# Adapter columns placed beside the output weights, their split made tile by tile, and the gathers put behind the first stage's weights

## The chip, the cores and the metric

The kernel runs on one core of one Trainium2 chip. The metric is device time in microseconds (us), the median of three runs. A profile of one execution, taken by the hardware profiler, shows what every engine did and when: TensorE (PE; its weight loads are PEld), VectorE (DVE), ScalarE (ACT), GpSimd (POOL) and SyncE (SP, which here only issues DMAs).

## The reference

Four layers, each added to its input x of shape 8 x 128 x 512 (B=8 rows, T=128 tokens, HID=512). All is in fp32.

```python
x = x + einsum('bsi,boi->bso', x, weight[adapter_ids])       # L0: one 512x512 weight of 8 for each row
x = x + attention(x)                                         # L1: 32 query heads in 8 groups (g), D=128
x = x + (x @ B_sel^T) @ A_sel^T                              # L2: rank 16
x = x + x @ W^T + b + 2 * lora(x)                            # L3: rank 16
def lora_linear(x, w, a, b, ids):                            # q, k, v and the output of L1 are of this form
    return x @ w + (x @ a[ids]) @ b[ids]                     # w: 512 x 4096 (q), 512 x 1024 (k, v), 4096 x 512 (output)
...
q, k = apply_rope(q), apply_rope(k)
p = softmax(causal_mask(q k^T / sqrt(128)))
o = (p v).reshape(B, T, 4096)
return lora_linear(o, wo, ao, bo, ids)                       # ao: 8 x 4096 x 16, selected per row b
```

## The kernel before

Every fp32 product is made of three matmuls in the format fp32r: an operand is split into a high part (a ScalarE copy that rounds) and a low part (a subtraction on VectorE or GpSimd), and high x high, low x high and high x low are summed in PSUM.

The program has four stages, each a block with a barrier at its end.

**First stage** (to 99 us): for each row b, TensorE transposes x and the row's own weight (five tiles of 128x512, L275), ScalarE and VectorE split them, TensorE multiplies (L286 to L288), VectorE adds the result to `res`, TensorE turns x1 (L296) and computes the adapters' inner products (L307 to L309) and turns these (L319). SyncE issues the weight of row b (1 MB, L225) into one of two buffers when the tiles of row b-2 have been transposed (`tile_ready`), then x of row b+1 and three adapter loads. GpSimd issues the gathers of the rows' adapters from HBM to HBM: 16 of 64 KB for keys and values (`bkv_sel`, L249 and L250), then 16 of 256 KB for queries and the output (`bq_sel`, `ao_sel`, L254 and L255); it starts as soon as the ids are there, and its part of the block ends when all have landed. Behind row b=4 SyncE waits for the small gathers and loads the first block of the second stage.

**Second stage** (to 229 us): keys and values. **Third stage** (to 766.8 us): attention, 8 heads g (each a group of four query heads) by 8 tiles b, 64 slots t = 8g + b. In a slot TensorE does, in this order: scores of t, a quarter of the queries of half a head (L81 to L86), turn of t-1 (four transposes, L1059), outputs of t-2, values of t-1 (L1067 to L1069). The order is written by hand and is the same in the heads 1 to 6, which are one loop body.

`outputs` (L1070 to L1092) multiplies the tile's attention result by the head's slice of wo: four query heads by three matmuls of 512 columns into `ps_out` (L1081 to L1083; each loads a 128x128 piece of `ot_hi` or `ot_lo` as its weights). Eight more matmuls (L1090, L1091) multiply the adapter slice `ao_pack` (high and low part side by side, 32 columns, as weights) into `ps_ao`. VectorE adds `ps_out` to `res` (L975) and `ps_ao` to `axo` (L976).

The slice of wo comes once a head: ScalarE rounds it head by head into `wo_hi` in slot b=1 (L844), after the last tile of the head before has been read (`out_ready`); VectorE subtracts two quarters (L962, in slots b=1 and b=2), GpSimd the other two (L932, in slot b=1) and behind them the low part of `ao_pack` (L935). GpSimd's other work in a slot: normalizing probabilities (L922), adding the two halves of rotated queries (L915), and in slots 0 to 3 splitting query weights (L907).

**Fourth stage** (to the end): the output's adapter product, L2 and L3. It begins with four matmuls (L1243) that spread `axo` over the partitions with a 0/1 matrix, `row_gather`.

Of the kernel before, what the change touches and what calls it, by code (L numbers as in the profile page):

```python
# [7 lines left out]
P = 128  # L8
F32 = mybir.dt.float32
# [21 lines left out]
def program(nc, x, lora_ids, pos, attn_ids, slot_ids, mask, w0, wq, wk, wv, wo, aq, bq, ak, bk, av, bv, ao, bo,  # L31
            l2a, l2b, w3, b3, l3a, l3b, ident_c, causal_c, rope_c, gather_c, twin_c, out):
# [34 lines left out]
    with whole:  # L67
# [22 lines left out]
        res = sb(whole, "res", [P, B, HID])  # L90
        ident = sb(whole, "ident", [P, P])
        ident_r = sb(whole, "ident_r", [P, P], F32R)
        axo = sb(whole, "axo", [2 * R, B, T])
# [3 lines left out]

        row_gather = sb(whole, "row_gather", [2 * R, 2, P])
# [55 lines left out]
        with ExitStack() as c:  # L154
# [51 lines left out]
            with nc.Block() as block:  # L206
                @block.sync
                def _(sp):
                    sp.dma_start(id_rows[:, 0, :], lora_ids.rearrange("(a b) -> a b", a=1)).then_inc(lora_ids_in, 16)
                    sp.dma_start(res[:, 0, :], x[0]).then_inc(x_in[0], 16)  # L210
                    sp.wait_ge(lora_ids_in, 16)
                    for b in range(B):
# [13 lines left out]
                        if b + 1 < B:  # L226
                            sp.dma_start(res[:, b + 1, :], x[b + 1]).then_inc(x_in[b + 1], 16)
# [12 lines left out]
                def _(pool):  # L240
# [19 lines left out]
                def _(pe):  # L260
                    def transposes(b):
# [3 lines left out]
                        for j in range(TILES):  # L265
# [7 lines left out]
                            for n in range(KC):  # L273
                                src = res[:, b, n * P:(n + 1) * P] if j == 0 else w0_raw[b % 2][:, n, (j - 1) * P:j * P]
# [16 lines left out]
                    def turn_x1(b):  # L291
# [3 lines left out]
                        for k in range(KC):  # L295
                            mm = pe.transpose(ps_x1[:, k, :], res[:, b, k * P:(k + 1) * P], ident[:, :])  # L296
# [94 lines left out]
                def _(dve):  # L391
# [8 lines left out]
                    def add(b):  # L400
                        dve.wait_ge(y_ready, b + 1)
                        dve.tensor_tensor(res[:, b, :], ps_y[b % 2][:, :], res[:, b, :], ALU.add).then_inc(x1_done, 1)
# [12 lines left out]
                    def pack_ax(b):  # L415
# [3 lines left out]
                        dve.wait_ge(zeroed, i + 1)  # L419
# [60 lines left out]

                    for i in range(2):
# [28 lines left out]
        ao_in = sem(late, "ao_in")  # L510
# [12 lines left out]
        def load_wo(dma, g):  # L523
            dma.dma_start(wo_raw[:, :, :], wo[bass.DynSlice(g * GW, GW), :].rearrange("(h p) n -> p h n", p=P)).then_inc(wo_in, 16)
            for b in range(B):
                dma.dma_start(ao_raw[:, b, :, :], ao_sel[b, bass.DynSlice(g * GW, GW), :].rearrange("(h p) r -> p h r", p=P)).then_inc(ao_in, 16)
# [8 lines left out]
        with ExitStack() as c:  # L535
# [24 lines left out]
            with nc.Block() as block:  # L560
                @block.sync
                def _(sp):
                    sp.wait_ge(first_packs, PAIRS)
                    load_block_b(sp, 1)
                    for n in range(BLOCKS * UNITS):
# [26 lines left out]
                        if n == VU:  # L592
                            load_wo(sp, 0)
                        if n == VU + 4:
# [124 lines left out]
        with ExitStack() as c:  # L719

            wq_raw, bq_raw, wq_hi, wq_lo, bq_pack = raw_w, raw_b, blk_hi[0], blk_lo[0], blk_b[0]
            wo_hi = sb(c, "wo_hi", [P, G, HID], F32R)
            wo_lo = sb(c, "wo_lo", [P, G, HID], F32R)
            ao_pack = sb(c, "ao_pack", [P, B, G, 2, R], F32R)
# [17 lines left out]
            ps_out = ps(c, "ps_out", [P, HID])  # L742
            ps_ao = ps(c, "ps_ao", [P, 512])
# [25 lines left out]
            axo_done = sem(c, "axo_done")  # L769
# [8 lines left out]
            with nc.Block() as block:  # L778
                @block.sync
                def _(sp):  # L780
                    def slots(g):
                        sp.wait_ge(wo_lo_done, G // 2 * (g + 1))
                        sp.wait_ge(wo_lo_pool, G // 2 * (g + 1))
                        sp.wait_ge(ao_lo_done, g + 1)
# [5 lines left out]
                        load_kv(sp, g + 1, 0)  # L790
                        sp.wait_ge(s_ready, B * g + B)
# [22 lines left out]

# [3 lines left out]
                    sp.dma_start(row_gather[:, :, :], gather_c).then_inc(w3_in, 16)  # L818
# [13 lines left out]
                def _(act):  # L832
# [10 lines left out]
                    def wo_hi_part(g, h):  # L843
                        act.activation(wo_hi[:, h, :], wo_raw[:, h, :], ACT.Copy).then_inc(wo_hi_done, 1)  # L844

                    def ao_hi_part(g):
                        act.wait_ge(ao_in, 16 * B * (g + 1))
                        act.activation(ao_pack[:, :, :, 0, :], ao_raw[:, :, :, :], ACT.Copy).then_inc(ao_hi_done, 1)
# [13 lines left out]
                    def slots(g, first, last):  # L862
                        for b in range(B):
                            t = B * g + b
                            number = t if first else None
# [26 lines left out]
                            if b == 1:  # L892
                                wo_hi_part(g, 1)
                                wo_hi_part(g, 3)
                                ao_hi_part(g)

                    over_heads(act, slots)
                    pt(B * KVH - 1, None)
                    ot(B * KVH - 1, None)

                @block.gpsimd
                def _(pool):
# [13 lines left out]

                    def slots(g, first, last):
                        for b in range(B):
                            t = B * g + b
                            i = b % 2  # L920
                            pool.wait_ge(inv_done, t + 1)
# [6 lines left out]
                            if b == 1:  # L928
                                for h in range(G // 2, G):

                                    pool.wait_ge(wo_hi_done, G * g + 2 * (h - G // 2) + 2)
                                    pool.tensor_tensor(wo_lo[:, h, :], wo_raw[:, h, :], wo_hi[:, h, :].bitcast(F32),  # L932
                                                       ALU.subtract).then_inc(wo_lo_pool, 1)
                                pool.wait_ge(ao_hi_done, g + 1)
# [527 lines left out]
```

## Time and profile before

| | us |
|---|---|
| median of three runs (lowest to highest) | 832.05 (831.7 to 832.5) |
| the profiled execution: its time | 832.55 |
| its span, first to last instruction | 830.9 |
| TensorE busy in the span | 771.7 (93%) |
| VectorE, ScalarE, GpSimd busy | 541.9, 324.5, 283.2 |
| mean granted clock of TensorE | 0.973 |

The difference of time and span, 1.65 us, lies before the first and after the last instruction. Busy times are sums over stages with different limits; for a stretch, the windows give the busy time of each engine in it, and a timeline gives each instruction with the idle time of its engine before it in brackets, and what ended that. TensorE's matmuls are pipelined, so that their durations overlap: what one costs is read from start to start.

### The profile page before, as it was taken

To read this page: it belongs to the slowest core of one execution; us is meant where nothing else is said; L and a number is where in the kernel's file an instruction comes from. 1 tells how busy PE (TensorE), PEld (TensorE's weight loads), DVE (VectorE), ACT (ScalarE), POOL (GpSimd) and SP (SyncE) were. 2 spreads that over 40 slices of the span, in tenths; PEclk is the share of its full clock that TensorE was granted. 3 is DMA by queue.
4 is the path that set the end of the run, shared out by engine and by line. 5 is a ranking of instruction groups with operands and counts; after the bars stand their busy time and mean duration, and the time that the engine had idled before them with its cause. 6 is when DMAs were issued, how large, how long until landed. Compare 5 with 4: busy or idle time off the path is not lost. (4 is left out here: it accounts for less than half of the span.)

```text
span 830.9 us, 13659 instructions
## 1 busy us (share of the span) xinstructions
PE 771.7 (93%) x4280; PEld 645.1 (78%) x4280; DVE 541.9 (65%) x1428; ACT 324.5 (39%) x924; POOL 283.2 (34%) x261
## 2 busy tenths in 40 slices
PE   4588897999789999999999999999999999988898
PEld 3477785778578888888888888888888888875686
DVE  2579542588665767677667667676767666754883
ACT  3255432311063445345335345435434543432550
POOL 5300020034455236227236326334523622420320
PEclk9889799999989999999999999999999999999899
DMA  9992187886405124213404402602512210710502
GB/s 270 348 262 57 56 214 211 239 229 191 139 2 141 37 65 109 70 49 78 114 0 120 120 0 65 165 10 63 133 43 63 64 38 13 153 16 8 124 19 84
DMA packets 112748, 86.86 MB, mean 105 GB/s; under 512 B 60534, under 2 KB 79126, under 8 KB 112454
## 3 DMA queue, kind: packets, MB, share of 16 engines
q1 hardware_dynamic: 110770, 79.83, 35.7%
q0 software_dynamic: 1792, 6.49, 2.3%
q8 instruction: 19, 0.31, 0.2%
q14 instruction: 19, 0.16, 0.1%
q10 hardware_dynamic: 148, 0.07, 0.0%
HBM read 71.40 MB, written 20.73 MB: 111 GB/s over the span
## 5 line engine op out<-in xcount | busy, mean ns | idle before, releaser
L922 POOL TENSOR_TENSOR prob<-prob,rinv 128x512 f32<-128x512 f32 x64 | 66.6, 1041 | 214.5 <-DVE rinv L1008 214.5
L871 ACT ACTIVATE prob<-sm,nmax 128x128 f32<-128x128 f32 x256 | 99.7, 391 | 77.9 <-DVE nmax L993 77.9
L1081 PE MATMUL ps_out<-wo_hi,ot_hi 128*128 128x512 f32 x256 | 106.5, 416 | 4.3 <-DVE ot_lo L970 2.4
L915 POOL TENSOR_TENSOR qt<-qc,qs 128x512 f32<-128x512 f32 x60 | 77.8, 1297 | 94.3 <-DVE qs L951 94.3
L860 ACT ACTIVATE ot_hi<-ps_o 128x512 fp32r<-128x512 f32 x64 | 38.1, 595 | 163.4 <-PE ps_o L1069 163.4
L1082 PE MATMUL ps_out<-wo_lo,ot_hi 128*128 128x512 f32 x256 | 100.7, 393 | 0.0
L1083 PE MATMUL ps_out<-wo_hi,ot_lo 128*128 128x512 f32 x256 | 100.6, 393 | 0.0
L81 PE MATMUL ps_q<-x1t_hi,blk_hi 128*128 128x512 f32 x240 | 100.4, 418 | 0.0
L82 PE MATMUL ps_q<-x1t_lo,blk_hi 128*128 128x512 f32 x240 | 95.3, 397 | 0.0
L83 PE MATMUL ps_q<-x1t_hi,blk_lo 128*128 128x512 f32 x240 | 95.1, 396 | 0.0
L951 DVE TENSOR_TENSOR qs<-ps_q,sin_t 64x512 f32<-64x512 f32 x120 | 82.7, 689 | 3.7
L993 DVE CUSTOM_DVE_ANT_0 sm<-ps_s,maskbias 128x128 f32<-128x128 f32 x256 | 59.0, 286 | 34.1 <-issue 33.5
L1051 PEld LDWEIGHTS ps_s<-kt,qt 128*128 128x128 f32 x512 | 67.7, 193 | 10.8 <-issue 5.4
L1051 PE MATMUL ps_s<-kt,qt 128*128 128x128 f32 x512 | 68.4, 277 | 5.2 <-PEq L560 5.2
L1081 PEld LDWEIGHTS ps_out<-wo_hi,ot_hi 128*128 128x128 f32 x256 | 48.1, 188 | 14.9 <-DVE ot_lo L970 4.0
L1083 PEld LDWEIGHTS ps_out<-wo_hi,ot_lo 128*128 128x128 f32 x256 | 48.0, 188 | 11.4
L990 DVE MEMSET gate<- 128x1 f32 x64 | 3.8, 59 | 79.8 <-PE ps_s L1051 79.8
L1082 PEld LDWEIGHTS ps_out<-wo_lo,ot_hi 128*128 128x128 f32 x256 | 48.3, 189 | 8.6
L854 ACT ACTIVATE pt_hi<-ps_t 128x512 fp32r<-128x512 f32 x64 | 38.1, 595 | 41.4 <-PE ps_t L1059 41.4
L83 PEld LDWEIGHTS ps_q<-x1t_hi,blk_lo 128*128 128x128 f32 x240 | 45.4, 189 | 11.0
L966 DVE TENSOR_TENSOR pt_lo<-ps_t,pt_hi 128x512 fp32r<-128x512 f32 x64 | 44.2, 691 | 13.4 <-ACT pt_hi L854 11.9
L82 PEld LDWEIGHTS ps_q<-x1t_lo,blk_hi 128*128 128x128 f32 x240 | 45.6, 190 | 8.3
(201 smaller groups left out, 1757.8 us busy)
## 6 DMA issues: line engine op xcount, KB each, us to landing
wo_raw<-in_L_cond_wo SPq DMA_DIRECT2D x8, 1024.0 KB, 5.3
raw_w<-in_L_cond_wq SPq DMA_DIRECT2D x8, 1024.0 KB, 6.5
w_raw<-in_L_cond_weight SPq DMA_DIRECT2D x7, 1024.0 KB, 6.9
raw_b<-bq_sel SPq DMA_DIRECT2D x56, 128.0 KB, 4.6
raw_b<-bkv_sel SPq DMA_DIRECT2D x16, 256.0 KB, 6.6
v_hi_d<-v_hi SPq DMA_DIRECT2D x16, 256.0 KB, 3.5
v_lo_d<-v_lo SPq DMA_DIRECT2D x16, 256.0 KB, 4.0
k_rot<-kr SPq DMA_DIRECT2D x16, 256.0 KB, 3.5
```

Of the source, the lines that this page charges most:

```text
L81: pe.matmul(bank[:, :], w_hi[:, k, cols], x1t_hi[:, k, tok], start=(k == 0), stop=False)
L82: pe.matmul(bank[:, :], w_hi[:, k, cols], x1t_lo[:, k, tok], start=False, stop=False)
L83: pe.matmul(bank[:, :], w_lo[:, k, cols], x1t_hi[:, k, tok], start=False, stop=False)
L871: e = act.activation(prob[i][:, h, :], sm[:, h, :], ACT.Exp, bias=nmax[i][:, h:h + 1], scale=-1.0, accum_out=rsum[i][:, h:h + 1])
L915: pool.tensor_tensor(qt[:, half, h, :], qc[:, :], qs[:, :], ALU.add).then_inc(q_done, 1)
L922: pool.tensor_tensor(prob[i][:, :, :], prob[i][:, :, :], rinv[i][:, :].unsqueeze(2).broadcast_to([P, G, T]), ALU.mult).then_inc(prob_done, 1)
L951: dve.tensor_tensor(qs[to:to + 64, :], ps_q[i][at:at + 64, :], sin_t[to:to + 64, tok], ALU.mult).then_inc(q_mult, 1)
L993: m = dve.tensor_tensor_reduce(out=sm[:, h, :], in0=ps_s[i][:, h, :], in1=maskbias[:, b, :], scale=-1.0, scalar=3.0e38, op0=ALU.add, op1=A ...
L1051: mm = pe.matmul(ps_s[b % 2][:, h, :], qt[:, half, h, at:at + T], kt[:, b * T:(b + 1) * T], start=True, stop=True)
L1081: pe.matmul(ps_out[:, :], ot_hi[:, q], wo_hi[:, h, :], start=(h == 0), stop=False)
L1082: pe.matmul(ps_out[:, :], ot_hi[:, q], wo_lo[:, h, :], start=False, stop=False)
L1083: pe.matmul(ps_out[:, :], ot_lo[:, q], wo_hi[:, h, :], start=False, stop=(h == G - 1))
```

## The change

- The adapters of the output become columns of the output weights. `wo_hi` and `wo_lo` have two halves of 264 columns: 256 of wo and 8 of the tile's adapter. `outputs` then is four heads by two halves by three matmuls of 264 columns, into two banks of `ps_out`; the eight matmuls into `ps_ao` are gone. `res` has the same form, its last 8 columns of each half gather the adapter sums, and one VectorE addition of 528 columns does both.
- The adapter columns belong to one tile: ScalarE writes their high part (`ao_hi_part`) and GpSimd their low part (`ao_lo_part`) for tile t-2 at the start of slot t, and TensorE waits for the low part (`ao_lo_done`) before the first matmul of `outputs`.
- ScalarE splits each quarter of wo as soon as TensorE has read that quarter for the last tile of the head before (`wo_head_read`); VectorE does both its quarters in slot b=1.
- GpSimd starts the small gathers when the weights of row b=3 are in, the large ones when those of all rows are. SyncE loads the second stage's first weights without waiting for a gather, its adapter rows behind the last row's loads.
- SyncE loads the adapters of the output for each tile apart, when the tile of the head before is done with them.
- The fourth stage spreads the adapter sums by four ScalarE and four VectorE copies into `axo_rows` and eight transposes, in place of `row_gather`.
- x is loaded and out stored in pieces of 1 KB, since a row of `res` has gaps.

```diff
-                        if b == 4:
-                            sp.wait_ge(gathered_kv, 2 * B * 16)
+                        if b == 4:
                             load_block_w(sp, 0)
-                            load_block_b(sp, 0)
+                    sp.wait_ge(gathered_kv, 2 * B * 16)
+                    load_block_b(sp, 0)
...
                     pool.wait_ge(ids_in, 32)
+                    pool.wait_ge(w0_in[1], 32)
                     for b in range(B):
...
+                    pool.wait_ge(w0_in[1], 64)
                     for b in range(B):
...
+                    dve.memset(res[:, :, :, WH:OW], 0.0).then_inc(zeroed, 1)
...
-            wo_hi = sb(c, "wo_hi", [P, G, HID], F32R)
-            wo_lo = sb(c, "wo_lo", [P, G, HID], F32R)
-            ao_pack = sb(c, "ao_pack", [P, B, G, 2, R], F32R)
+            wo_hi = sb(c, "wo_hi", [P, G, 2, OW], F32R)
+            wo_lo = sb(c, "wo_lo", [P, G, 2, OW], F32R)
...
+            def adapter(b):
+
+                return ao_raw[:, b, :, :].rearrange("p h (a r) -> p h a r", a=2)
...
                     def slots(g):
+                        if not isinstance(g, int) or g >= 1:
+                            sp.wait_ge(ao_lo_done, B * g)
+                            adapters(g, B - 2, B)
...
                         load_kv(sp, g + 1, 0)
+                        sp.wait_ge(ao_lo_done, B * g + B - 2)
+                        adapters(g + 1, 0, B - 2)
...
+                    def wo_hi_part(g, h, first):
+                        if not first:
+                            if h < G - 1:
+                                act.wait_ge(wo_head_read, (G - 1) * (B * g - 1) + h + 1)
+                            else:
+                                act.wait_ge(out_ready, B * g)
+                        act.activation(wo_hi[:, h, :, 0:WH], halves(wo_raw[:, h, :]), ACT.Copy).then_inc(wo_hi_done, 1)
+
+                    def ao_hi_part(t, g, b):
+
+                        act.wait_ge(ao_in[b], 16 * (g + 1))
+                        if not isinstance(t, int) or t >= 1:
+                            act.wait_ge(out_ready, t)
+                        act.activation(wo_hi[:, :, :, WH:OW], adapter(b), ACT.Copy).then_inc(ao_hi_done, 1)
...
                         for b in range(B):
                             t = B * g + b
-                            number = t if first else None
+                            if not first or b >= 2:
+                                ao_hi_part(t - 2, g - 1 if b < 2 else g, (b - 2) % B)
...
-                                if not first:
-                                    act.wait_ge(out_ready, B * g)
-                                wo_hi_part(g, 0)
-                                wo_hi_part(g, 2)
+                                for h in range(G):
+                                    wo_hi_part(g, h, first)
...
+                    def ao_lo_part(t, b):
+                        pool.wait_ge(ao_hi_done, t + 1)
+                        pool.tensor_tensor(wo_lo[:, :, :, WH:OW], adapter(b), wo_hi[:, :, :, WH:OW].bitcast(F32),
+                                           ALU.subtract).then_inc(ao_lo_done, 1)
...
+                            if not first or b >= 2:
+                                ao_lo_part(t - 2, (b - 2) % B)
                             pool.wait_ge(inv_done, t + 1)
...
-                        dve.tensor_tensor(res[:, b, :], ps_out[:, :], res[:, b, :], ALU.add).then_inc(res_done, 1)
-                        dve.tensor_tensor(axo[:, b, :], ps_ao[0:2 * R, 0:T], axo[:, b, :], ALU.add).then_inc(axo_done, 1)
+                        dve.tensor_tensor(res[:, b, :, :], ps_out[:, :, 0:OW], res[:, b, :, :], ALU.add).then_inc(res_done, 1)
...
-                            if b == 2:
-                                wo_lo_part(g, 1)
...
                             if b == 1:
                                 wo_lo_part(g, 0)
+                                wo_lo_part(g, 1)
...
+                        pe.wait_ge(ao_lo_done, t + 1)
                         for h in range(G):
...
-                            pe.matmul(ps_out[:, :], ot_hi[:, q], wo_hi[:, h, :], start=(h == 0), stop=False)
-                            pe.matmul(ps_out[:, :], ot_hi[:, q], wo_lo[:, h, :], start=False, stop=False)
-                            pe.matmul(ps_out[:, :], ot_lo[:, q], wo_hi[:, h, :], start=False, stop=(h == G - 1))
-                        if b == 0:
-                            pe.wait_ge(ao_lo_done, g + 1)
-                        pe.wait_ge(axo_done, t + 1)
...
+                            for a in range(2):
+                                o = ps_out[:, a, 0:OW]
+                                pe.matmul(o, ot_hi[:, q], wo_hi[:, h, a, :], start=(h == 0), stop=False)
+                                pe.matmul(o, ot_hi[:, q], wo_lo[:, h, a, :], start=False, stop=False)
+                                mm = pe.matmul(o, ot_lo[:, q], wo_hi[:, h, a, :], start=False, stop=(h == G - 1))
+                            mm.then_inc(wo_head_read if h < G - 1 else out_ready, 1)
...
-                        pe.matmul(ps_h[i][:, :], row_gather[:, i, :], axo[:, i:B:2, :], start=True, stop=True).then_inc(axo_ready, 1)
+                        pe.wait_ge(axo_spread[i], 4)
+                        for b in range(i, B, 2):
+                            mm = pe.transpose(ps_h[i][:, b // 2 * T:(b // 2 + 1) * T], axo_rows[:, b, :, :, :].rearrange("p q i r -> p (q i r)"),
+                                              ident[:, :])
+                        mm.then_inc(axo_ready, 1)
```

TensorE in a slot of the loop body, from the last transposes to the first values of the next tile (`ps_t` holds the turned probabilities, `ps_o` the values). Before:

```order
L1059 MATMUL ps_t<-ident,prob 128x128 x3
L1081 MATMUL ps_out<-wo_hi,ot_hi 128x512 [waits res_done,ot_lo_done]
L1082 MATMUL ps_out<-wo_lo,ot_hi 128x512
L1083 MATMUL ps_out<-wo_hi,ot_lo 128x512
...
L1090 MATMUL ps_ao<-ot_hi,ao_pack 32x128 [waits axo_done]
L1091 MATMUL ps_ao<-ot_lo,ao_pack 32x128
...
L1067 MATMUL ps_o<-pt_hi,v_hi 128x512 [waits ot_lo_done,pt_lo_done,v_in0]
```

And after:

```order
L1095 MATMUL ps_t<-ident,prob 128x128 x3
L1120 MATMUL ps_out<-wo_hi,ot_hi 128x264 [waits ao_lo_done,res_done,ot_lo_done]
L1121 MATMUL ps_out<-wo_lo,ot_hi 128x264
L1122 MATMUL ps_out<-wo_hi,ot_lo 128x264
...
L1103 MATMUL ps_o<-pt_hi,v_hi 128x512 [waits ot_lo_done,pt_lo_done,v_in0]
```

The three 512-column rows stood four times, the pair into `ps_ao` four times; the three 264-column rows stand eight times. The wait for the adapter split stands at the first matmul of every tile.

GpSimd in the loop body, from the query work of slot b=1 to the probabilities of slot b=2. Before:

```order
L915 TENSOR_TENSOR qt<-qc,qs 128x512 [waits s_ready,q_mult]
L905 REGISTER_ALU
L907 TENSOR_TENSOR blk_lo<-raw_w,blk_hi 128x4x128 [waits wq_hi_done]
L932 TENSOR_TENSOR wo_lo<-wo_raw,wo_hi 128x512 [waits wo_hi_done]
L931 REGISTER_ALU
L932 TENSOR_TENSOR wo_lo<-wo_raw,wo_hi 128x512 [waits wo_hi_done]
L934 REGISTER_ALU
L935 TENSOR_TENSOR ao_pack<-ao_raw,ao_pack 128x32x16 [waits ao_hi_done]
L921 REGISTER_ALU
L922 TENSOR_TENSOR prob<-prob,rinv 128x512 [waits inv_done]
```

And after:

```order
L947 TENSOR_TENSOR qt<-qc,qs 128x512 [waits s_ready,q_mult]
L937 REGISTER_ALU
L939 TENSOR_TENSOR blk_lo<-raw_w,blk_hi 128x4x128 [waits wq_hi_done]
L970 REGISTER_ALU
L971 TENSOR_TENSOR wo_lo<-wo_raw,wo_hi 128x2x256 [waits wo_hi_done]
L970 REGISTER_ALU
L971 TENSOR_TENSOR wo_lo<-wo_raw,wo_hi 128x2x256 [waits wo_hi_done]
L951 TENSOR_TENSOR wo_lo<-ao_raw,wo_hi 128x8x8 [waits ao_hi_done]
L960 REGISTER_ALU
L961 TENSOR_TENSOR prob<-prob,rinv 128x512 [waits inv_done]
```

The split of the adapters of a whole head, behind the two splits of output weights, has become that of one tile (b=0), in the same place; the other tiles' stand ahead of the probabilities of later slots.

GpSimd in the first stage, at the first of the small gathers. Before:

```order
L244 DMA rope_cols<-in_rope_c 128x3
L247 TENSOR_LOAD id_rows [waits ids_in]
L247 ISA x2
L249 ISA
L249 DMA bkv_sel<-in_L_cond_bk 16x1024
```

And after, with the first of the large ones too:

```order
L250 DMA rope_cols<-in_rope_c 128x3
L254 TENSOR_LOAD id_rows [waits w0_in1,ids_in]
L254 ISA x2
L256 ISA
L256 DMA bkv_sel<-in_L_cond_bk 16x1024
...
L260 TENSOR_LOAD id_rows [waits w0_in1]
L260 ISA x2
L262 ISA
L262 DMA bq_sel<-in_L_cond_bq 16x4096
```

Nothing moved against its neighbours on this engine; two waits for the second weight buffer (`w0_in1`) are added, and all that GpSimd issues in this stage stands behind them.

## Rows read from the trace of the kernel before

**Rows 1.** Windows: us, busy PE PEld DVE ACT POOL (count), clock, DMA, GB/s
```profile
300.00:363.00 63.00, 63.00 (x374) 53.37 (x373) 42.81 (x137) 26.35 (x83) 27.35 (x22) 1.00 0.30 80
...
729.00:768.00 39.00, 32.72 (x192) 25.60 (x191) 17.95 (x66) 13.30 (x45) 4.16 (x4) 1.00 0.07 7
```

**Rows 2.** TensorE timeline, a slot: start, us, operation, count [idle before]
```profile
506.70 0.40 PE L86 MATMUL ps_q<-axt_q,blk_b 128*128 128x256 f32 x2
...
506.94 0.60 PE L1059 MATMUL ps_t<-ident,prob 128*128 128x128 f32 x4
...
507.30 0.47 PE L1081 MATMUL ps_out<-wo_hi,ot_hi 128*128 128x512 f32 x1
...
507.61 0.39 PE L1082 MATMUL ps_out<-wo_lo,ot_hi 128*128 128x512 f32 x1
...
510.16 0.22 PE L1090 MATMUL ps_ao<-ot_hi,ao_pack 128*32 128x128 f32 x1
...
510.63 0.45 PE L1067 MATMUL ps_o<-pt_hi,v_hi 128*128 128x512 f32 x1
```

**Rows 3.** Timeline of TensorE, first outputs of a head
```profile
515.67 0.47 PE L1081 MATMUL ps_out<-wo_hi,ot_hi 128*128 128x512 f32 x1
```

**Rows 4.** Timeline of TensorE in the first stage
```profile
17.52 3.67 PE L275 MATMUL ps_ring<-ident,w_raw 128*128 128x128 f32 x16 [2.93 <-DMA w_raw<-in_L_cond_weight]
...
30.44 0.60 PE L275 MATMUL ps_ring<-ident,res 128*128 128x128 f32 x4
...
39.55 3.68 PE L275 MATMUL ps_ring<-ident,w_raw 128*128 128x128 f32 x16 [8.51 <-DMA w_raw<-in_L_cond_weight]
...
52.06 1.71 PE L275 MATMUL ps_ring<-ident,w_raw 128*128 128x128 f32 x8 [1.89 <-DVE xt_lo L398]
...
59.43 0.62 PE L275 MATMUL ps_ring<-ident,res 128*128 128x128 f32 x4
...
75.44 0.62 PE L275 MATMUL ps_ring<-ident,res 128*128 128x128 f32 x4
```

**Rows 5.** Timeline of the queues of SyncE and GpSimd in the first stage
```profile
24.38 3.08 SPq L225 DMA_DIRECT2D w_raw<-in_L_cond_weight  x1
...
30.66 0.49 POOL L255 DMA_DIRECT2D ao_sel<-in_L_cond_ao  x1
```

**Rows 6.** Windows in the first stage and behind a wait in the last head
```profile
35.00:45.60 10.60, 6.05 (x23) 5.38 (x24) 3.79 (x5) 2.39 (x4) 0.00 (x0) 0.52 0.94 297
...
52.40:55.80 3.40, 3.40 (x13) 2.78 (x12) 2.84 (x5) 1.19 (x2) 0.00 (x0) 0.50 1.03 321
...
732.00:736.00 4.00, 3.79 (x22) 3.16 (x23) 1.36 (x5) 1.63 (x7) 1.04 (x1) 1.00 0.27 28
```

**Rows 7.** Timeline of GpSimd, second slot of a head
```profile
511.67 1.75 POOL L907 TENSOR_TENSOR blk_lo<-raw_w,blk_hi 128x512 fp32r<-128x512 f32 x1
...
513.37 3.17 POOL L932 TENSOR_TENSOR wo_lo<-wo_raw,wo_hi 128x512 fp32r<-128x512 f32 x2
...
516.51 1.29 POOL L935 TENSOR_TENSOR ao_pack<-ao_raw,ao_pack 128x512 fp32r<-128x512 f32 x1
```

**Rows 8.** Timeline of GpSimd and TensorE in the first head
```profile
246.25 3.01 POOL L932 TENSOR_TENSOR wo_lo<-wo_raw,wo_hi 128x512 fp32r<-128x512 f32 x2
...
246.94 0.47 PE L1081 MATMUL ps_out<-wo_hi,ot_hi 128*128 128x512 f32 x1
```

**Rows 9.** TensorE timeline: last head's wait, fourth stage's start
```profile
732.21 0.47 PE L1081 MATMUL ps_out<-wo_hi,ot_hi 128*128 128x512 f32 x1 [1.63 <-DVE res L975]
...
766.81 1.95 PE L1243 MATMUL ps_h<-axo,row_gather 32*128 32x512 f32 x4 [1.25 <-PEq L778]
```

**Rows 10.** Groups of instructions by form: busy us, mean ns | idle before
```profile
L1081 PEld LDWEIGHTS ps_out<-wo_hi,ot_hi 128*128 128x128 f32 x256 | 48.1, 188 | 14.9 <-DVE ot_lo L970 4.0 <-issue 1.8 <-POOL wo_lo L932 0.5
```

**Rows 11.** Timeline of TensorE, the adapters' matmuls of the first stage
```profile
57.72 0.27 PE L307 MATMUL ps_a<-a_hi,x1t_hi 128*128 128x48 f32 x1
...
57.83 0.27 PE L308 MATMUL ps_a<-a_lo,x1t_hi 128*128 128x48 f32 x1
```

More of the change, by code:

```diff
@@ L273, in transposes @@
                             for n in range(KC):
-                                src = res[:, b, n * P:(n + 1) * P] if j == 0 else w0_raw[b % 2][:, n, (j - 1) * P:j * P]
+                                src = row(b, n) if j == 0 else w0_raw[b % 2][:, n, (j - 1) * P:j * P]
                                 mm = pe.transpose(ps_ring[m % 3][:, n * P:(n + 1) * P], src, ident[:, :])
@@ L401, in add @@
                         dve.wait_ge(y_ready, b + 1)
-                        dve.tensor_tensor(res[:, b, :], ps_y[b % 2][:, :], res[:, b, :], ALU.add).then_inc(x1_done, 1)
+                        own = res[:, b, :, 0:WH]
+                        dve.tensor_tensor(own, ps_y[b % 2][:, :].rearrange("p (a n) -> p a n", a=2), own, ALU.add).then_inc(x1_done, 1)
                     def split_x1(b):
@@ L509, in program @@
         bq_in = [sem(late, f"bq_in{i}") for i in range(2)]
-        ao_in = sem(late, "ao_in")
+        ao_in = [sem(late, f"ao_in{b}") for b in range(B)]
         kt_in = [sem(late, f"kt_in{i}") for i in range(2)]
@@ L593, in _ @@
                             load_wo(sp, 0)
+                            for b in range(B):
+                                load_ao(sp, 0, b)
                         if n == VU + 4:
@@ L780, in _, with adapters @@
                 def _(sp):
+                    def adapters(g, first, last):
+                        for b in range(first, last):
+                            load_ao(sp, g, b)
                     def slots(g):
+                        if not isinstance(g, int) or g >= 1:
+                            sp.wait_ge(ao_lo_done, B * g)
+                            adapters(g, B - 2, B)
                         sp.wait_ge(wo_lo_done, G // 2 * (g + 1))
                         sp.wait_ge(wo_lo_pool, G // 2 * (g + 1))
-                        sp.wait_ge(ao_lo_done, g + 1)
                         load_wo(sp, g + 1)
@@ L1153, in program @@
             bias_in = sem(c, "bias_in")
+            axo_spread = [sem(c, f"axo_spread{i}") for i in range(2)]
             axo_ready = sem(c, "axo_ready")
@@ L1270, in _ @@
                         pe.wait_ge(wide_done, b + 1)
-                        turn(X2 + b, [res[:, b, k * P:(k + 1) * P] for k in range(KC)])
+                        turn(X2 + b, [row(b, k) for k in range(KC)])
                     pe.wait_ge(m_done, PAIRS)
@@ L1307, in pack_hi @@
                             act.activation(pack[at:at + 32, both, :], own[n % 2][:, :, :], ACT.Copy).then_inc(h_hi_done, 1)
+                    for quad in range(4):
+                        to, of = spread(0, quad)
+                        act.activation(to, of, ACT.Copy).then_inc(axo_spread[0], 1)
                     act.wait_ge(l2_in, 32 * B)
@@ L1363, in low_half @@
                         dve.tensor_tensor(pack[low, pair, :], raw[low, pair, :], pack[low, pair, :].bitcast(F32), ALU.subtract).then_inc(lo_done, 1)
+                    for quad in range(4):
+                        to, of = spread(1, quad)
+                        dve.tensor_copy(to, of).then_inc(axo_spread[1], 1)
                     dve.wait_ge(l2a_hi_done, 1)
@@ L1387, in _ @@
                     for b in range(B):
-                        add(b, res[:, b, :])
+                        add(b, res[:, b, :, 0:WH])
                     for b in range(B):
@@ L1409, in _ @@
                         dve.wait_ge(bias_done, b + 1)
-                        add(B + b, res[:, b, :])
+                        add(B + b, res[:, b, :, 0:WH])
                 @block.gpsimd
@@ L1439, in constants @@
     causal = np.where(np.tril(np.ones((P, P), bool)), 0.0, NEG).astype(np.float32)
-    row, col = np.arange(2 * R_PACK)[:, None], np.arange(P)[None, :]
     twin = np.stack([(np.arange(P) // R_PACK) % 2 == i for i in range(2)] + [-(np.arange(P) // (2 * R_PACK) % 2)], 1).astype(np.float32)
-    gather = np.stack([(row % R_PACK == col % R_PACK) & (col // R_PACK % 2 == i) for i in range(2)], 1).astype(np.float32)
-    return {"ident_c": np.eye(P, dtype=np.float32), "causal_c": causal, "rope_c": rope, "gather_c": gather, "twin_c": twin}
+    return {"ident_c": np.eye(P, dtype=np.float32), "causal_c": causal, "rope_c": rope, "twin_c": twin}
 def kernel(**inputs):
```

77 lines of the change are left out of this document (36 added, 41 removed).

## The prediction

> **What bounds the kernel now.** I read the busy time by stretch first. In the middle of attention TensorE is busy 63.00 of 63.00 us at the full granted clock, while VectorE works 42.81, ScalarE 26.35 and GpSimd 27.35 of them [rows 1]: there a TensorE instruction saved is time saved, and work put on the other three costs only where TensorE comes to wait for it. In the last head, where no queries are left to compute, TensorE works 32.72 of 39.00 us [rows 1] and a chain of softmax steps sets the pace. Then the timeline of one slot: outputs run from 507.30 to 510.63, twelve matmuls of 512 columns and eight of 128 [rows 2], and the next slot's outputs start at 515.67 [rows 3], a slot of 8.37 us. Last the first stage: TensorE starts the transposes of a batch row at 30.44, gets its weights at 39.55 after 8.51 us of waiting for their DMA, and later rows start at 59.43 and 75.44, 16.0 us for two [rows 4].
>
> **First stage.** The two rows between 30.44 and 59.43 took 29.0 us where the two behind them took 16.0 [rows 4]. The weights (1 MB) came late because 4 MB of large gathers stood beside them: SyncE's issue at 24.38 lasts 3.08 us, and GpSimd issues the last gather at 30.66 [rows 5]. Behind the wait the clock is low as well: 0.52 on average from 35.0 to 45.6, 0.50, the level of 1.2 GHz, from 52.4 to 55.8 [rows 6]. The change holds the small gathers back until the weights of b=3 are in, the large ones until all are. Weights of b=3 then meet only the loads of their own rows, and I take the steady period of 8.0 us for all: 29.0 − 16.0 = 13.0 off. What is late next is VectorE's split of a transposed tile, as at 52.06 [rows 4]; that is in the 8.0. Lower bound: the 8.51 of waiting alone, less some delay from the small gathers, 8; upper: 16, if the 2.93 us of wait before b=1's weights at 17.52 [rows 4] go too. The 4 MB at 297 GB/s [rows 6] are 14 us, twice that if other loads take half; begun near 50 they end between 64 and 78, and the stage ends near 86 in place of 99, so their wait at the block's end costs nothing. If that cover went, they would hold the barrier.
>
> **Columns.** From 507.61 eleven 512-column matmuls take 2.55 us, 0.232 each; the eight of 128 take 0.47 [rows 2]. After it a tile has 24 of 264 columns: 6336 in place of 7168. Two matmuls of 256 columns, each with its own 128x128 weights, take 0.24 [rows 2], 0.120 each; from 512 columns in proportion a 264 costs 0.1195, from 256 in proportion 0.124. I take 0.1205. With the 0.08 that the first of a run costs more (0.31 to the second, [rows 2]): 24 × 0.1205 + 0.08 = 2.97, against 3.33 now, 0.36 a tile (0.28 to 0.38). Four tiles of the last head lie on the softmax chain and gain nothing; 60 × 0.36 = 21.6 us (17 to 23).
>
> The Trainium skill (TensorE: Matmul & The Clock Gate, section "Wait — 56ns, not 53.3ns?") puts the gap of a warm matmul at N/2.4 + 2.5 ns; by that 24 of 264 cost 2.70 and the present set 3.04, a gain of 0.34 a tile and 20 us. This trace has 232 ns for 512 where the rule says 216, so the rows stand.
>
> **The adapter split.** It was one GpSimd instruction a head, needed only by the last eight matmuls of the tile; now GpSimd splits the adapters of every tile, and TensorE waits for that before the first matmul of outputs. The new 128x8x8 operation is in no row: at most the 1.29 of the 128x512 form [rows 7], at least its eighth, 0.16. I take 0.25. In most slots GpSimd is idle when it comes up, and ScalarE's counterpart lies in its idle time: nothing. Not in the second slot of a head. There GpSimd's queue holds the split of query weights at 511.67, two splits of output weights from 513.37 that end at 516.54 [rows 7], and only then the new one, ending at 516.8. TensorE comes to these outputs at 515.67 [rows 3], by the shorter outputs before them at 515.31. So it waits 1.5 us, in the six heads 1 to 6: +9.0. If the query-weight split takes 1.29 and not 1.75, 1.0; if the new operation takes 1.29, 2.55. Queued behind it on TensorE are the values of the previous tile, and so ScalarE's and VectorE's splits of them. In the last head there is no split of query weights and no wait. In the first, the splits run from 246.25 for 3.01, the new one to 249.5, and TensorE is there at 246.94 [rows 8]: 2.55 of wait, against 0.75 that it waits now for the old split (246.25 + 3.01 + 1.29 = 250.55, where the twelve matmuls before it would end at 249.80, 2.86 after their start as in [rows 2]): +1.8. A stall of 1.89 us at 52.06 [rows 4] was followed by half clock for 3.4 us [rows 6], one of 1.63 at 732.21 [rows 9] was not [rows 6]; so I add 1.7 once, for the first head, and none for the six.
>
> **Everything else.** VectorE loses 64 small adds, and both its splits now stand in one slot; it has 20 us of 63 free [rows 1]: nothing. ScalarE splits output weights as each head has been read, earlier than now: nothing, GpSimd is what comes last. Fourth stage: eight 128-column transposes, 0.72 by the four that take 0.36 in [rows 2], for four matmuls that take 1.95 us [rows 9]; before them stand four small copies on each of two engines, which no row shows, at most four of the 1.29 form [rows 7] less the 1.25 that TensorE idles there now: −1.2 to +2.7, I take +0.3. SyncE's adapter loads spread over the head lie two slots ahead of use: nothing. x and out in pieces of 1 KB: nothing, unless the first stage is bound by DMA again (in its lower bound).
>
> **Sum.** From the profiled execution of 832.55 (its span of 830.9 and 1.65 around it, which nothing here touches): −13.0 − 21.6 + 9.0 + 1.8 + 1.7 + 0.3 = 810.75. The median of the runs, 832.05, is 0.5 lower: 810.
>
> **Rivals.** *No wait at the heads' second slot.* VectorE and GpSimd may run the splits earlier because ScalarE's halves come head by head. For it: the first head is read a quarter into the 3.33 us of outputs [rows 2]. Against: GpSimd has no gap between 511.67 and 517.8 [rows 7], it is bound by its own work. Time: 810.3 − 12.5 = 798. *Longer waits.* The new split costs 1.29 whatever its size, 2.55 six times (+6.3), or the waits bring half clock after them (up to 1.7 each, +10): 816 to 826, say 822. Against: 1.63 us at 732.21 cost no clock. *The first stage gains nothing.* DMA goes on to bind it, or the large gathers hold the barrier: 810 + 13 = 823. Against: the period of 8.0 us holds in the stretch without gathers, with no DMA wait. *Slower: weight loads set the spacing.* A 264-column matmul has half the time of a 512 to hide its 128x128 load, and there are 24 loads where there were 12 (and eight small ones). A load's row lasts 188 ns [rows 10]; if loads don't overlap one another, 24 × 0.188 + 0.08 = 4.59, +1.26 a tile, +76 over 60, the waits vanish: 832.55 − 13.0 + 76 − 0.5 = 895. It decides from a spacing of 0.135 us on, where a tile costs what it does now. Against it: matmuls of 48 columns with such loads start 0.11 apart [rows 11], and the pair of 256 is 0.120 apart; but they are pairs, not runs of 24.
>
> The Trainium skill (TensorE: Matmul & The Clock Gate, section "The mechanism" of its Part 3) says that a weight load overlaps with matmuls in flight only when its row group differs. All these loads use every row; by that rule load and matmul would follow one another, and the time would be on the side of the 895. In this trace the 0.11 of [rows 11] and 0.120 of [rows 2] are shorter than one load's row alone, so it is not so here.
>
> **Chances.** The forecast 0.53 (its own range 805 to 817); no wait 0.13; longer waits 0.12; first stage without gain 0.12; slower by loads 0.07; two of the bad ones together, no change, 0.03. Two tenths of a per cent, 1.7 us, is what a measurement of this kernel can tell from no change: faster 0.90, same 0.03, slower 0.07. The range 796 to 826 takes in all but the last two and some of the edges.
>
> **What would show it.** Right: first-stage period 8.0 from b=3 on, no wait above 2 us for weights past 25 us; outputs of a steady tile in 2.95 to 3.0 us and a slot of 8.0; six waits of 1 to 2 us of TensorE on GpSimd's adapter split at the outputs of b=0, one of 2.5 in the first head; half clock once. Wrong: 264-column matmuls more than 0.13 apart; slots without queries' work growing; the barrier of the first stage released by a gather; the clock low after each of the six waits.

## The result, and the profile after

The changed kernel takes 810.4 us (median of four runs, 806.7 to 812.2) against 832.3 for the kernel before: a ratio of 0.974 (95% interval 0.971 to 0.977). The forecast was 810. The profiled execution took 809.34, its span is 807.6. The stages begin, in TensorE's timeline of the kernel before (start, us, operation, in brackets the idle time), here for the second and third, with the fourth in [rows 9]:

```profile
99.25 0.77 PE L701 MATMUL ps_p<-blk_hi,x1t_hi 128*128 128x512 f32 x1 [0.97 <-PEq L206]
...
229.49 1.83 PE L1051 MATMUL ps_s<-kt,qt 128*128 128x128 f32 x7 [5.20 <-PEq L560]
```

And in the same view of the changed kernel, for the second, third and fourth:

```profile
90.00 0.77 PE L714 MATMUL ps_p<-blk_hi,x1t_hi 128*128 128x512 f32 x1 [0.97 <-PEq L212]
...
218.56 1.84 PE L1087 MATMUL ps_s<-kt,qt 128*128 128x128 f32 x7 [5.19 <-PEq L571]
...
744.75 1.09 PE L1280 MATMUL ps_h<-ident,axo_rows 128*128 128x128 f32 x8 [1.81 <-ACT axo_rows L1351]
```

| us | before | after | difference | in the sum |
|---|---|---|---|---|
| first stage, to the first projection | 99.25 | 90.00 | −9.25 | −13.0 |
| second stage | 130.24 | 128.56 | −1.7 | 0 |
| attention, first scores to first matmul of the fourth stage | 537.3 | 526.2 | −11.1 | −21.6 + 9.0 + 1.8 + 1.7 = −9.1 |
| fourth stage, to the end of the span | 64.1 | 62.8 | −1.2 | +0.3 |

So the total came out, and its terms did not: the first stage gave 3.7 us less than forecast, and the other three stages 5.2 us more. The slot first, TensorE in the changed kernel; the columns are start, duration, engine, line, operation and count:

```profile
491.11 0.60 PE L1095 MATMUL ps_t<-ident,prob 128*128 128x128 f32 x4
491.47 0.37 PE L1120 MATMUL ps_out<-wo_hi,ot_hi 128*128 128x264 f32 x1
...
494.45 0.40 PE L1103 MATMUL ps_o<-pt_hi,v_hi 128*128 128x512 f32 x1
...
499.08 0.60 PE L1095 MATMUL ps_t<-ident,prob 128*128 128x128 f32 x4
501.07 0.38 PE L1120 MATMUL ps_out<-wo_hi,ot_hi 128*128 128x264 f32 x1 [1.40 <-POOL wo_lo L951]
```

Outputs take 2.98 us (491.47 to 494.45) in place of 3.33 [rows 2], for 24 matmuls. The next outputs, of a new head's first tile, begin 1.40 us after TensorE had nothing else left, and the profile names GpSimd's split. Its queue, which answers to [rows 7]:

```profile
494.59 1.78 POOL L947 TENSOR_TENSOR qt<-qc,qs 128x512 f32<-128x512 f32 x1 [2.01 <-DVE qs L990]
496.32 1.75 POOL L939 TENSOR_TENSOR blk_lo<-raw_w,blk_hi 128x512 fp32r<-128x512 f32 x1
498.04 2.52 POOL L971 TENSOR_TENSOR wo_lo<-wo_raw,wo_hi 128x512 fp32r<-128x512 f32 x2
500.51 0.33 POOL L951 TENSOR_TENSOR wo_lo<-ao_raw,wo_hi 128x64 fp32r<-128x64 f32 x1
```

The adapter split (L951) stands behind both weight quarters, ends at 500.84, and costs 0.33 us. Over the kernel (engine, line waited for, us in total, times, longest):

```profile
PE ps_out L1120 <- POOL wo_lo L951: 8.4, 6, 1.4
```

Six waits, 1.4 each. The first head has one more. The profile gives it no releaser but TensorE's own issue; GpSimd's split ends at 239.32, just ahead of the matmul:

```profile
239.42 0.36 PE L1120 MATMUL ps_out<-wo_hi,ot_hi 128*128 128x264 f32 x1 [2.41 <-issue]
239.00 0.32 POOL L951 TENSOR_TENSOR wo_lo<-ao_raw,wo_hi 128x64 fp32r<-128x64 f32 x1
```

The windows of the changed kernel (busy us of PE, PEld, DVE, ACT, POOL; clock; DMA) answer to [rows 1, 6]:

```profile
16.00:22.60 6.60, 5.47 (x21) 4.97 (x22) 3.21 (x5) 2.39 (x4) 0.00 (x0) 0.50 1.15 279
...
43.30:46.60 3.30, 3.30 (x11) 2.79 (x11) 2.72 (x5) 1.19 (x2) 0.00 (x0) 0.51 0.48 78
300.00:363.00 63.00, 61.60 (x408) 56.07 (x407) 43.08 (x133) 28.35 (x96) 27.75 (x30) 1.00 0.30 79
704.00:744.00 40.00, 32.84 (x241) 29.75 (x239) 18.89 (x62) 14.18 (x50) 8.27 (x12) 1.00 0.09 11
```

TensorE lacks 1.40 us of full work in 300 to 363, which hold one such wait; the last head still idles 7.2 of 40. In the first stage, which answers to [rows 4]:

```profile
30.66 0.60 PE L283 MATMUL ps_ring<-ident,res 128*128 128x128 f32 x4
...
39.19 0.66 PE L283 MATMUL ps_ring<-ident,res 128*128 128x128 f32 x4
...
42.61 1.71 PE L283 MATMUL ps_ring<-ident,w_raw 128*128 128x128 f32 x8 [1.89 <-DVE xt_lo L406]
...
50.06 0.62 PE L283 MATMUL ps_ring<-ident,res 128*128 128x128 f32 x4
...
66.11 0.62 PE L283 MATMUL ps_ring<-ident,res 128*128 128x128 f32 x4
```

Before, row b=3 started at 30.44 [rows 4] and b=4 18.2 us behind it:

```profile
48.64 0.66 PE L275 MATMUL ps_ring<-ident,res 128*128 128x128 f32 x4
```

Now b=3 starts at 30.66, its weights are there, and b=4 follows after 8.53 us. But b=5 comes 10.87 us after b=4; the two rows behind that take 16.05. The issues (answering to [rows 5]) show why b=3 is not held up: its weights are asked for ahead of all gathers, the small gathers start at 28.20, and the last large one is issued at 75.28. Their data is in by 79.8, 10 us ahead of the second stage.

```profile
20.98 0.38 SPq L231 DMA_DIRECT2D w_raw<-in_L_cond_weight  x1
...
28.20 0.51 POOL L256 DMA_DIRECT2D bkv_sel<-in_L_cond_bk  x1 [24.40 <-issue]
...
75.28 0.49 POOL L263 DMA_DIRECT2D ao_sel<-in_L_cond_ao  x1
```

### The profile page after: what moved, and what is told of

The parts are those of the page before. It is cut to its first block and busy times, and to the rows that moved or that the text cites. A ratio compares the mean times of both kernels' runs of the same rounds, so it can differ in the third digit from the quotient of the medians.

```text
span 807.6 us, 14320 instructions
## 1 busy us (share of the span) xinstructions
PE 739.2 (92%) x4540; PEld 651.3 (81%) x4540; DVE 537.2 (67%) x1368; ACT 331.8 (41%) x984; POOL 293.4 (36%) x318
## 5 line engine op out<-in xcount | busy, mean ns | idle before, releaser
L1120 PE MATMUL ps_out<-wo_hi,ot_hi 128*128 128x264 f32 x512 | 150.8, 295 | 15.2 <-POOL wo_lo L951 8.4
L1122 PE MATMUL ps_out<-wo_hi,ot_lo 128*128 128x264 f32 x512 | 145.3, 284 | 0.0
L1121 PE MATMUL ps_out<-wo_lo,ot_hi 128*128 128x264 f32 x512 | 144.9, 283 | 0.0
L947 POOL TENSOR_TENSOR qt<-qc,qs 128x512 f32<-128x512 f32 x60 | 80.9, 1348 | 102.6 <-DVE qs L990 102.6
L1120 PEld LDWEIGHTS ps_out<-wo_hi,ot_hi 128*128 128x128 f32 x512 | 96.6, 189 | 18.6 <-issue 14.6
L1121 PEld LDWEIGHTS ps_out<-wo_lo,ot_hi 128*128 128x128 f32 x512 | 96.7, 189 | 0.0
L1122 PEld LDWEIGHTS ps_out<-wo_hi,ot_lo 128*128 128x128 f32 x512 | 96.0, 187 | 0.0
```

Source lines behind the costliest of these rows:

```text
L947: pool.tensor_tensor(qt[:, half, h, :], qc[:, :], qs[:, :], ALU.add).then_inc(q_done, 1)
L1120: pe.matmul(o, ot_hi[:, q], wo_hi[:, h, a, :], start=(h == 0), stop=False)
L1121: pe.matmul(o, ot_hi[:, q], wo_lo[:, h, a, :], start=False, stop=False)
L1122: mm = pe.matmul(o, ot_lo[:, q], wo_hi[:, h, a, :], start=False, stop=(h == G - 1))
```

## The experiments

**Gathers early again.** The changed kernel without the two waits for `w0_in[1]` on GpSimd, and with the second stage's first loads behind the small gathers again:

```diff
-                    pool.wait_ge(w0_in[1], 32)
...
-                    pool.wait_ge(w0_in[1], 64)
```

> The changed kernel with its gathers issued at the start again, as in the kernel before (and the second stage's first weights behind the small gathers); the rest of the change stays. If the gathers made the long wait for b=3's weights, that wait of some 8.5 us is back, the first stage ends near 99 us instead of 90, and the time is 809.3 + 9.3 = 818 to 819. Rival: the wait went because of the other edits to that stage (x in pieces, the zeroing): then the stage ends near 90 and the time stays near 810. The attention stage should be as in the changed kernel: 526 us, with six waits of 1.4 us on GpSimd's adapter split.

820.1 us (ratio to before 0.985, 0.981 to 0.989). TensorE waits 8.80 us for the weights of b=3 and the second stage starts at 98.06; the attention has its six periods of 9.61 us:

```profile
40.89 3.55 PE L281 MATMUL ps_ring<-ident,w_raw 128*128 128x128 f32 x16 [8.80 <-DMA w_raw<-in_L_cond_weight]
...
98.06 0.77 PE L712 MATMUL ps_p<-blk_hi,x1t_hi 128*128 128x512 f32 x1 [0.97 <-PEq L212]
```

So it is the early gathers that make that wait, and not the other edits to this stage (the loads put back with them stand behind b=4's on SyncE); between these two profiles the stage differs by 8.1 us.

**Gathers late alone.** The kernel before with only the same waits added, and the second stage's first loads in the order of the change:

> The kernel before with only the gathers put behind the first-stage weights (and the second stage's first loads reordered as in the change). If the two parts of the change add up, the first stage is 9.2 us shorter and the rest unchanged: 832.3 - 9.2 = 823. By the term of the prediction it would be 13.0 shorter, 819. If the gathers only move their cost to a later place (the barrier, or a slower second stage), 828 to 832.

821.3 us (0.986, 0.982 to 0.990). The second stage starts at 89.02, and all periods of the attention but the last head's are 8.37. The two halves of the change nearly add up: from 832.3, the gathers alone take 11.0 us off, the rest alone 12.2 (the run above), and both together 21.9 of these 23.2, where the runs of one kernel lie up to 7 us apart. And the stage is 10.2 us shorter, not 13.0.

**Large gathers late, small ones early.** The changed kernel without the first of the two waits only:

> The changed kernel with its small gathers (16 of 64 KB) issued at the start again; only the large ones (16 of 256 KB) wait for the weights of all rows. If it was the large gathers that held up b=3's weights, TensorE waits no longer than now for weights (3.8 and 3.3 us in the first two rows, none at b=3), the second stage starts near 90 us, and the time is that of the changed kernel, 810. If the small ones count in proportion to their 1 MB, a fifth of the 5 MB, some 2 us of the 9.3 come back: 812. In the run with all gathers early the wait before b=3 was 8.8 us.

812.5 us (0.977, 0.975 to 0.980); the second stage starts at 90.53, and before b=3 there is no wait for weights. So it was the 4 MB of large gathers that held them up. What the small ones cost stays open: the stage is 0.5 us longer in this profile, but profiles of the same first stage differ by 1.1 (90.00, 89.98, and 88.87 in the run with the first tile's adapters ahead), and the median is 3.2 above that of the changed kernel measured beside it (809.3, the last run below), where 2 were expected if the small ones count by their size.

**The sine table early.** Both profiles have one row, b=4, that takes 10.8 us, and in both TensorE waits 1.89 for VectorE's split of the transposed x [rows 4]. What that split waited for is on ScalarE, in the kernel before:

```profile
48.44 1.28 ACT L381 ACT_TABLE_LOAD   x1
```

And in the changed kernel:

```profile
38.99 1.28 ACT L389 ACT_TABLE_LOAD   x1
40.29 1.06 ACT L389 ACTIVATE sin_t<-ang 128x1024 f32<-128x1024 f32 x1
41.25 0.58 ACT L353 ACTIVATE xt_hi<-ps_ring 128x512 fp32r<-128x512 f32 x1
```

A table of the activation function is loaded, then 1024 sines a partition are computed for the rotation, and only then comes the split that TensorE needs. The experiment makes ScalarE compute one sine at the start, so that the first table it loads is that one:

```diff
+                    act.activation(sin_t[:, 0:1], ident[:, 0:1], ACT.Sin)
                     act.activation(ident_r[:, :], ident[:, :], ACT.Copy).then_inc(ident_ready, 1)
```

> The changed kernel with one element of a sine computed on ScalarE before its first copy, so that the sine table is loaded at the start and not in row b=4. In both profiles the row that follows the sine takes 10.8 us where others take 8.0: ScalarE loads a table (1.28 us) and computes 1.06 us of sines ahead of the split of the transposed x, TensorE waits 1.89 us for that, and its clock is at half for 3.4 us behind. If the table load is what makes it, TensorE's wait there falls to about 0.6 us and the row takes 9.5, or 8.2 if the half clock goes too: 1.3 to 2.7 us off, 808 to 809. Rival (what the prediction took): the row is long because of the DMA of the weights: then it stays at 10.8.

806.6 us (0.970, 0.967 to 0.974), 3.8 under the 810.4 of the changed kernel. ScalarE in this run, at its start and in row b=4:

```profile
2.13 1.28 ACT L376 ACT_TABLE_LOAD   x1 [2.13 <-issue]
...
38.45 1.05 ACT L390 ACTIVATE sin_t<-ang 128x1024 f32<-128x1024 f32 x1
39.52 0.60 ACT L353 ACTIVATE xt_hi<-ps_ring 128x512 fp32r<-128x512 f32 x1
```

TensorE in the same row, and the start of the next:

```profile
38.77 0.65 PE L283 MATMUL ps_ring<-ident,res 128*128 128x128 f32 x4
...
40.90 1.25 PE L283 MATMUL ps_ring<-ident,w_raw 128*128 128x128 f32 x8 [0.60 <-DVE xt_lo L407]
...
46.82 0.62 PE L283 MATMUL ps_ring<-ident,res 128*128 128x128 f32 x4
```

The changed kernel too loads a table at 2.13, for its first copy. With the sine ahead of that copy row b=4 has no load: the sines are followed by the split at once, the wait is 0.60, and the row takes 8.05 us (38.77 to 46.82). The second stage starts at 86.77, 3.2 earlier, of which 2.8 are this row. The window of this row has the full clock (1.00, where the changed kernel has 0.51 behind its wait of 1.89):

```profile
38.00:47.00 9.00, 8.40 (x62) 7.42 (x62) 8.42 (x18) 5.13 (x10) 1.95 (x4) 1.00 1.00 319
```

So the prediction's reading of b=4 was wrong: neither its wait nor the half clock behind it came from the weights. The run with all gathers early parts the two. Its row b=4 has the wait, the full clock behind it (1.00 from 52 to 56), and takes 9.35 us (48.73 to 58.08):

```profile
52.15 1.25 PE L281 MATMUL ps_ring<-ident,w_raw 128*128 128x128 f32 x8 [1.90 <-DVE xt_lo L404]
```

So of the 2.8 us, 1.3 are the wait and 1.5 the clock.

**The first tile's adapters ahead of the weight quarters.** In slot b=1 ScalarE and GpSimd split them as soon as the previous tile's outputs are done, and not at the start of slot b=2:

```diff
                                     wo_hi_part(g, h, first)
+                                ao_hi_part(t - 1, g, 0)
...
                             if b == 1:
+                                ao_lo_part(t - 1, 0)
                                 for h in range(G // 2, G):
```

> The changed kernel with the adapter split of a head's first tile made at the end of slot b=1, on ScalarE behind the four weight quarters, on GpSimd ahead of its two quarters, instead of behind them at the start of slot b=2. If GpSimd's queue is what TensorE waits for, the six waits of 1.4 us and the 2.4 us of the first head go: each of the six periods of 9.61 us falls to 7.97, 9.8 in all, 2 in the first head, 0.4 in the last: 810.4 - 12 = 798. Rival: the wait moves on to GpSimd's two quarters, which now end 0.3 us later, at 500.9 by the present trace, while TensorE would need them at 500.9 and 501.7: then 0.1 to 0.5 remain of each. Rival: what sets the period there is VectorE, whose two quarters delay the scores: then the periods stay near 9.6 and the time near 810.

797.4 us (0.959, 0.955 to 0.962), as expected. GpSimd's timeline at the second slot of the same head:

```profile
489.96 0.32 POOL L952 TENSOR_TENSOR wo_lo<-ao_raw,wo_hi 128x64 fp32r<-128x64 f32 x1
490.24 2.55 POOL L973 TENSOR_TENSOR wo_lo<-wo_raw,wo_hi 128x512 fp32r<-128x512 f32 x2
```

TensorE's there:

```profile
491.00 0.60 PE L1097 MATMUL ps_t<-ident,prob 128*128 128x128 f32 x4
491.36 0.37 PE L1122 MATMUL ps_out<-wo_hi,ot_hi 128*128 128x264 f32 x1
```

The new split ends at 490.28, the outputs follow the transposes at once (491.36), and the two quarters, done at 492.79, are in time for the query heads that need them: no wait of TensorE on GpSimd is left, and every period from the first head's second tile into the last head is 7.97 to 8.00 us. The rival that VectorE's two quarters set the pace is out.

**Both edits.**

> The changed kernel with both edits that the runs so far point to: the adapter split of a head's first tile ahead of the weight quarters, and the sine table loaded at the start. Alone they took 13.0 us (797.4) and, in the first stage's end, 3.2 us (86.8 in place of 90.0) off. If they are independent the time is 797.4 - 3.2 = 794, with the attention's periods at 7.97 us throughout and the second stage starting near 87. If not, 797.

794.6 us (792.6 to 797.3; ratio 0.956, 0.954 to 0.959), the second stage from 86.82, all periods behind the first 7.97 to 8.00 up to the last tiles. The two gains add up (2.8 us under the 797.4 above), and this version beats both kernels as measured beside it: 14.6 us under the changed one (809.3, the next run) and 36.6 under the one before it (831.2).

**The changed kernel once more.**

> The changed kernel unaltered, on the same chip as the two runs beside it, as their standard: 807 to 812, with the second stage at 90 us and six periods of 9.61 us. Its runs differ by 5 us so far; if that is the granted clock, this profile shows half-speed stretches in other places than the first one, and stage times that differ from it by about half the length of those stretches.

809.3 us (0.974, 0.972 to 0.977). Its first stage is that of the first profile (89.98), its six periods too. What differs is the first head and the second stage: at the start of the attention TensorE waits 2.42 us for the first adapter split in this profile, and 2.41 in the other. Behind it the windows differ (the last three columns are clock, DMA and GB/s). In this one, with most of the stretch at the lower level:

```profile
240.50:243.80 3.30, 3.30 (x20) 3.30 (x19) 0.57 (x1) 0.00 (x0) 2.59 (x3) 0.59 0.88 305
```

In the first profile, at the full clock:

```profile
240.20:243.70 3.50, 3.50 (x29) 3.37 (x28) 0.61 (x1) 0.41 (x1) 2.64 (x3) 1.00 0.89 296
```

From the first outputs to the second it is 9.48 us here (239.69 to 249.17) and 7.95 there. The runs with the sine, with all gathers early and with the small ones early have 9.48 or 9.49 as well. The same wait costs 1.5 us of clock in four of five profiles.

## Why the prediction was right, and where it was not

*The bottleneck in attention, and the columns (−21.6).* Right. The slot without a wait is 7.97 us, 0.40 less, where 0.36 was forecast: 0.35 are the 24 matmuls at 0.121 start to start (0.1205 was taken), and 0.05 more comes from the values behind them. Their first matmul of 512 columns started the second 0.29 after it where it followed the eight 128-column matmuls; now it is 0.23. The tiles in sum: 56 slots at 0.402 and three of the tail's at 0.43, −23.8.

*The wait in six heads (+9.0).* Right in place, mechanism and size: 1.40 us each and a period 1.64 longer than the others, 9.8 in all. The new GpSimd operation took 0.33 for the 0.25 taken. The queue ahead of it was another than the one added up, and two differences nearly cancelled: the query add took 1.78 in place of 1.29, and the two weight quarters 1.26 each in place of 1.58. VectorE's two quarters, which both stand in this slot now, run beside the query add and the query-weight split and no longer beside GpSimd's quarters. The prediction put that move at nothing; that it came to little is luck.

*The first head (+1.8 and +1.7 of clock).* The wait was 2.41 for 2.55, and it goes when the split is moved ahead. The clock behind it fell in four profiles of five, but not in the one of the table: there the way from the first scores to the second tile's outputs is 28.8 us (218.56 to 247.37) against 26.6 (229.49 to 256.10), a net of +2.2 for 3.5. As a term it was likely, not certain.

*The last head (0).* Its period at the same place is 8.39, +0.4, with a wait of 0.2. It is the same split: with that moved ahead the period is 7.97. So "no wait" in the last head was wrong too, by little.

*The first stage (−13.0): here a step failed.* The 9.25 lie within its bounds of 8 and 16, but the term was mis-sized. The prediction took "the two rows between 30.44 and 59.43" as one consequence of late weights and gave both back the steady 8.0. One row's excess of 10 was that (18.2 to 8.53, and back with 8.80 of wait when the gathers were early). The other's 2.8 belonged to ScalarE's sine table, and stayed: 10.79 before, 10.87 after, 8.05 with the table loaded early. The row that the prediction quoted, 1.89 behind `xt_lo`, had the pointer in it, and was counted as "in the 8.0". Nor did the first two rows gain anything: their waits for weights are 3.84 and 3.30 where they were 4.27 and 2.93, though the gathers were gone, and from 16.0 to 22.6 the clock is 0.50 where it was 1.00 before.

*The cover of the gathers.* It held, by less than forecast: they began at 63.24, not at 50, since the last row's weights land at about that time, and their data was in 10 us ahead of the second stage.

*The second and fourth stages (0 and +0.3).* They took 1.7 and 1.2 us less. TensorE's instructions in the second stage are the same. In the profile before, two stretches inside it, away from its ends, run at half clock; in the profile after, none does. The repeated profile of the changed kernel has one there and 129.1 us for that stage, the version with both edits two and 131.0. So this part of the gain is of the execution, not of the change. Before:

```profile
131.00:134.30 3.30, 2.82 (x7) 2.26 (x8) 1.72 (x3) 1.00 (x2) 0.00 (x0) 0.50 0.79 229
185.50:189.00 3.50, 3.50 (x10) 2.76 (x9) 2.43 (x3) 2.00 (x4) 1.29 (x1) 0.51 1.05 397
```

The same stretches after:

```profile
131.00:134.30 3.30, 3.30 (x16) 2.66 (x15) 1.15 (x2) 1.36 (x3) 0.00 (x0) 1.00 0.66 197
185.50:189.00 3.50, 3.50 (x17) 2.86 (x17) 3.37 (x6) 0.00 (x0) 0.03 (x1) 1.00 0.99 238
```

In the fourth stage part is of the change: the eight transposes take 1.09 us where the four matmuls took 1.95 [rows 9], but the wait before them, which the table counts under attention, is 1.81 where it was 1.25. That is −0.3 for the forecast +0.3. The mean clock of that stage is 1.00 for 0.95; that the other 0.4 us come of it is not shown.

*The rivals.* "Weight loads set the spacing" is out: 24 matmuls with 24 loads of 188 ns each follow one another at 0.12. The loads overlap. "No wait at the second slot" would have been true with another order of two instructions on GpSimd. "The first stage gains nothing" is out. So is "longer waits", except for the first head's clock.

What agreed in the total is thus partly luck: a first stage that gave 3.7 less was made up by the clock (1.7 in the second stage, 1.3 in the first head, where it did not fall), by the columns (2) and by the fourth stage (1.5, of which 0.9 are the transposes).

## What to carry to other kernels

Where an instruction is put last in another engine's queue, add up that queue from its anchor to its end and compare with the time at which the waiting engine arrives; here this gave a wait of 1.5 us, measured 1.4, and moving one instruction ahead of two, with the ScalarE copy that it needs, took it away. When a stall is removed, check each slow period behind it for its own releaser before giving it back the steady pace. And take a difference in a stage without changed work as the size of what single profiles can differ by.

## What the runs showed of the hardware

VectorE and GpSimd held each other up where both computed from SBUF to SBUF. In the kernel before VectorE's quarter took 0.67 us, and GpSimd's weight quarter beside it 1.92, where the one ahead of that took 1.29:

```profile
514.72 0.67 DVE L962 TENSOR_TENSOR wo_lo<-wo_raw,wo_hi 128x512 fp32r<-128x512 f32 x1
514.62 1.92 POOL L932 TENSOR_TENSOR wo_lo<-wo_raw,wo_hi 128x512 fp32r<-128x512 f32 x1
```

In the changed kernel two such quarters stand in a row on VectorE, at the query add on GpSimd; the second row shows the second quarter by itself:

```profile
494.54 2.38 DVE L1001 TENSOR_TENSOR wo_lo<-wo_raw,wo_hi 128x512 fp32r<-128x512 f32 x2
495.15 1.76 DVE L1001 TENSOR_TENSOR wo_lo<-wo_raw,wo_hi 128x512 fp32r<-128x512 f32 x1
```

The first took 0.69, the query add 1.78 in place of 1.29, and the second quarter 1.76. The Trainium skill (SBUF — State Buffer, section "🔬 SBUF: two separate sides") calls the port pair that the two share an exclusive lock, taken by GpSimd and by a VectorE operation with two SBUF inputs. These rows nearly agree: before, the longer GpSimd quarter is its own 1.29 and 0.63 of VectorE's 0.67; after, a quarter, the query add and a quarter need 0.69 + 1.29 + 0.69 = 2.67 us one behind another, and the two engines are at it from 494.54 to 496.92, 2.38 us. Where the 0.29 less comes from no run here shows.

And the same 2.4 us wait, at the same place of the same program, brought half clock behind it in four profiles of five and none in the fifth.
